# Ten value products of the second wide attention, moved into the rounds of the token attention

## The reference

```
# layer 1, ffn: token attention (16 heads of 8, keys are the 256 tokens), then 8 experts
x = x + layernorm(attention(x, Wq, bq, Wk, bk, Wv, bv, Wo, bo), ln1_g, ln1_b)
x = x + layernorm(moe(x, gate_w, gate_b, W1, b1, W2, b2), ln2_g, ln2_b)
# layer 2, attention: 16 heads of 64, keys and values from the context
xn = layernorm(x, ln_gamma, ln_beta)
q = xn @ w_q
k, v = split(context @ w_kv)
attn = softmax(q * SCALE @ k.T)
out = (attn @ v) @ w_out + b_out
```

## Time and profile before

| | us |
|---|---|
| median of three runs | 602.95 |
| profiled execution | 600.79 |
| its span | 598.7 |
| TensorE busy | 527.3 |
| VectorE busy | 449.2 |
| ScalarE busy | 344.9 |
| POOL busy | 217.3 |

### The profile page before, as it was taken

One profiled execution on the slowest core, in us unless ns is written; L12 is line 12 of the kernel. 1 busy time (PEld: TensorE's weight loads), 2 busy tenths in 40 slices (PEclk: granted clock), 3 DMA queues, 4 the chain that ended last, 5 costly groups with the idle time before them and its releaser, 6 DMA issues.

```text
span 598.7 us, 13027 instructions
## 1 busy us (share of the span) xinstructions
PE 527.3 (88%) x4784; PEld 304.3 (51%) x4792; DVE 449.2 (75%) x1251; ACT 344.9 (58%) x672; POOL 217.3 (36%) x214
## 2 busy tenths in 40 slices
PE   8889999997878799988996789688999999898896
PEld 3345555555843123333333467435666566754584
DVE  5989999998368679927876799867777776496653
ACT  3578888887144156644751768448888878222112
POOL 2047777778120000000002547206777778200100
PEclk9989999999999779999998999989999999999969
DMA  8770000004010000000000211000000000000000
GB/s 220 144 210 2 3 1 2 2 2 142 2 36 0 2 1 2 1 2 2 1 1 18 88 54 54 2 1 1 1 2 2 2 2 2 2 1 1 1 0 19
DMA packets 24082, 15.40 MB, mean 26 GB/s; under 512 B 8083, under 2 KB 22230, under 8 KB 23894
## 3 DMA queue, kind: packets, MB, share of 16 engines
q1 hardware_dynamic: 24022, 14.60, 9.2%
HBM read 14.33 MB, written 0.26 MB: 24 GB/s over the span
## 4 chain that ended last, share of the span: by engine, by line
PE 40%; issue 29%; DVE 18%; ACT 9%; POOL 3%; DMA 0%; DVEq 0%; POOLq 0%; ACTq 0%
PE psM L433 4%; PE pspair L483 3%; DVE Zt L1524 3%; ACT PP L1181 3%; PE pspair L632 3%; PE pspair L885 2%; PE psS L457 2%; PE psO L657 2%; PE psO L501 2%; DVE Oall L1782 2%; PE psS L405 2%; PE pspair L373 2%; DVE Oall L1572 1%; ACT PP L1165 1%; PE pspair L405 1%
## 5 line engine op out<-in xcount | busy, mean ns | idle before, releaser
L2193 POOL TENSOR_TENSOR ln_rs<-ln_ve,minus_half 128x4 f32<-128x4 f32 x10 | 10.2, 1023 | 225.0 <-DVE ln_ve L1411 221.8
L483 PE MATMUL pspair<-ident,PP 128*128 128x128 f32 x528 | 84.0, 282 | 7.8 <-ACT PP L1181 4.3
L483 PEld LDWEIGHTS pspair<-ident,PP 128*128 128x128 f32 x528 | 57.4, 140 | 50.5 <-issue 41.9
L501 PE MATMUL psO<-V,PP 128*128 128x64 f16 x1536 | 65.0, 193 | 11.7 <-DVE Oall L1572 9.8
L501 PEld LDWEIGHTS psO<-V,PP 128*128 128x128 f16 x1536 | 60.3, 98 | 17.1 <-DVE PP L1537 13.4
L1537 DVE TENSOR_TENSOR PP<-pspair,PP 128x512 f16<-128x512 f32 x68 | 46.8, 688 | 27.5 <-ACT PP L1165 27.4
L1239 ACT ACTIVATE PP<-pspair 128x1024 f32<-128x1024 f32 x48 | 46.6, 1023 | 30.3 <-PE pspair L643 30.2
L1181 ACT ACTIVATE PP<-scores_m,nm 128x512 f32<-128x512 f32 x68 | 49.5, 728 | 17.5 <-DVE nm L1511 13.9
L2202 POOL TENSOR_TENSOR PP<-acc,one 128x512 f16<-128x512 f32 x32 | 33.3, 1039 | 72.0 <-ACT acc L1163 71.8
L1165 ACT CAST PP<-pspair 128x512 f16<-128x512 f32 x68 | 39.6, 583 | 4.5 <-PE pspair L483 4.5
L2202 POOL TENSOR_TENSOR PP<-y_sb,one 128x512 f16<-128x512 f32 x32 | 33.3, 1039 | 19.5 <-ACT y_sb L1163 19.4
(11 more groups left out here) (497 smaller groups left out, 1224.8 us busy)
## 6 DMA issues: line engine op xcount, KB each, us to landing
W<-in_L_ffn_W SPq DMA_DIRECT2D x16, 256.0 KB, 2.9
bigw<-in_L_xattn_w_q SPq DMA_DIRECT2D x2, 512.0 KB, 5.7
bigw<-in_L_xattn_w_kv SPq DMA_DIRECT2D x1, 1024.0 KB, 5.6
V<-in_ctx SPq DMA_DIRECT2D x1, 512.0 KB, 3.9
bigw<-in_L_xattn_w_v SPq DMA_DIRECT2D x1, 512.0 KB, 5.9
mask_b<-in_mask_BxS_ff SPq DMA_DIRECT2D x1, 512.0 KB, 8.1
bigw<-in_L_xattn_w_k SPq DMA_DIRECT2D x1, 512.0 KB, 6.4
bigw<-in_L_xattn_w_o SPq DMA_DIRECT2D x1, 512.0 KB, 4.0
```

The source lines that it names most:

```text
L483: mm = pe.transpose(bank[f"T{j % 2}"][:, k * P:(k + 1) * P], Pb[j % 4][:, k * P:(k + 1) * P], ident[:])
L501: mm = pe.matmul(bank["O"][:, (j % UPH) * a.dv:(j % UPH + 1) * a.dv], (PTH, PTL)[ppart][j % 4][:, k * P:(k + 1) * P], values_of(a)[vpart][ ...
```

## The change

Products 6 to 15 are no longer made in `pe_l2x`. They are made in the rounds of the token attention, at the end of TensorE's order in the round, through the ring: one in each of rounds 0 to 5 and two in rounds 6 and 7 (`LATE_VALUES`). ScalarE, at the end of its order in the round, copies the product whole, in fp32, to one of two tiles of `scores_m` (`V32`), and that frees the bank. From the third of these copies on it first waits until POOL has split the product two before. POOL forms both halves from the fp32 copy, with two operations like those that it has for probabilities: a multiplication by one that rounds to fp16, and a subtraction. All ten splits stand in POOL's order ahead of the reciprocal root of the norm that follows the token attention. VectorE's ten subtractions are gone, and so are ScalarE's ten roundings. Ahead of the wide attention's rounds TensorE waits for all ten splits.

```diff
--- before.py
+++ after.py
@@ -93,6 +93,7 @@
 HR = P // HG
 VR = DN + 1
 MSCALE = 64.0
+LATE_VALUES = {0: (6,), 1: (7,), 2: (8,), 3: (9,), 4: (10,), 5: (11,), 6: (12, 13), 7: (14, 15)}
 L1X = Packed("L1x", SK, mask=True)
 L1F = Packed("L1f", S, scale=float(DN) ** -0.5)
 
@@ -308,6 +309,7 @@
         KW = maskf.bitcast(F16)
         zero_m = [Zt[:].bitcast(BF16)[:, k * SK:(k + 1) * SK] for k in range(2)]
         P32 = [t[:].rearrange("p t d -> p (t d)") for t in (acc, y_sb)]
+        V32 = [Sm[2], Sm[3]]
         Kst = [KW, Amat[:, 0:8, :].rearrange("p a c -> p (a c)").bitcast(F16)]
         K32 = tmp[:].rearrange("p t d -> p (t d)")
         minus16 = G[:, 0, 0, :].bitcast(F16)
@@ -538,6 +540,8 @@
                     scores(0, j)
             for v in last_v:
                 emptied(pe, v)
+            if a is L2X:
+                pe.wait_ge(sem("L2.vsplit"), 2 * NC - 6)
             run(pe, a, rounds)
             nr = a.units // UPI
             for j in range(a.lag, 0, -1):
@@ -704,6 +708,10 @@
                     turn_out(g - 1)
                 if r + a.lead < a.rounds:
                     natural(r + a.lead, 1)
+                for v in LATE_VALUES.get(r, ()) if not a.mask else ():
+                    ps, done = ring(pe, a, f"L2.V{v}")
+                    pe.matmul(ps[:], ctxT[:, v // 2 * P:(v // 2 + 1) * P], bigw[:, 2, v % 2 * 512:(v % 2 + 1) * 512],
+                              start=True, stop=True).then_inc(done, 1)
 
         def pe_out(pe, a, W, chunks):
 
@@ -906,11 +914,10 @@
             rounds(E // 2 - 1, True)
 
         def pe_l2x(pe):
-            pe_wide_values(pe, "L2", range(6, 2 * NC))
             pe_first_keys(pe, L2X, ctxT, "ld.L2")
             pe_ln(pe, "L2x", XN[1])
             pe_first_query(pe, L2X, XT[1])
-            pe_attention(pe, L2X, ctxT, XT[1], [f"L2.V{v}" for v in range(2 * NC)])
+            pe_attention(pe, L2X, ctxT, XT[1], [f"L2.V{v}" for v in range(6)])
             pe.wait_ge(sem("ld.L2wo"), 16)
             pe_out(pe, L2X, lambda c: bigw[:, 3, c * P:(c + 1) * P], NPAIR)
 
@@ -1258,6 +1265,11 @@
                     if g > 1:
                         filled(act, f"{n}.ot{g - 2}")
                     nc.scalar.copy(Osb, bank["O"][:]).then_inc(sem(f"{n}.out"), 1)
+                for v in LATE_VALUES.get(r, ()) if not a.mask else ():
+                    ps = filled(act, f"L2.V{v}")
+                    if v >= 8:
+                        act.wait_ge(sem("L2.vsplit"), v - 7)
+                    nc.scalar.copy(V32[v % 2], ps[:]).then_inc(free_of(f"L2.V{v}"), 1)
 
         def act_out(act, a, chunks):
             for c in range(0, chunks, 2):
@@ -1343,7 +1355,6 @@
             act_out(act, L1F, 1)
             act_copy(act, "L1g.xt", XT[0][:])
             act_moe(act)
-            act_wide_values(act, "L2", range(6, 2 * NC))
             act_first_keys(act, L2X)
             act_copy(act, "L2x.xt", XT[1][:])
             act_first_query(act, L2X)
@@ -1870,14 +1881,12 @@
                 add_up(E // 2 - 1, 1)
                 emptied(dve, "moe.y1", E // 2 - 1)
                 dve.wait_ge(sem("L1g.added"), 2)
-                ln_gain("L1gn", acc, "L1_ffn_ln2_g", lambda t: X[:, t, :], X, "L1gn.xn", lows("L2", range(6, 7)))
+                ln_gain("L1gn", acc, "L1_ffn_ln2_g", lambda t: X[:, t, :], X, "L1gn.xn")
                 dve.wait_ge(sem("L1gn.xn"), NT)
 
             def l2x():
                 ln_gain("L2b", X, "L2_xattn_ln_gamma", lambda t: rowp["L2_xattn_ln_beta"], XN[1], "L2x.xn",
-                        lows("L2", range(7, 8)), twice_normed=True)
-                for step in lows("L2", range(8, 16)):
-                    step()
+                        twice_normed=True)
                 first_keys(L2X)
                 first_query(L2X)
                 attention(L2X)
@@ -2272,6 +2281,18 @@
             selectors()
             rstd("L1x")
             rstd("L1f")
+
+            def split_values(v):
+                emptied(pool, f"L2.V{v}")
+                cols_ = slice(v % 2 * 512, (v % 2 + 1) * 512)
+                pool.tensor_tensor(VH[:, v // 2, cols_], V32[v % 2], one[:].broadcast_to([P, 512]), ALU.mult)\
+                    .then_inc(sem("L2.vhigh"), 1)
+                pool.wait_ge(sem("L2.vhigh"), v - 5)
+                pool.tensor_tensor(VL[:, v // 2, cols_], V32[v % 2], VH[:, v // 2, cols_], ALU.subtract)\
+                    .then_inc(sem("L2.vsplit"), 1)
+
+            for v in range(6, 2 * NC):
+                split_values(v)
             rstd("L1fn")
 
             def split_W2(i, k2, first):
```

## The result

The changed kernel took 614.02 us (median of four runs, 612.31 to 618.75), the kernel before 603.43 us (four runs, 601.65 to 603.97). The ratio is 1.0198, 95% interval 1.0155 to 1.024: slower, by an amount of which it is not clear whether it is above 2%. Ratios and their intervals leave out runs that took over 1.5% longer than the fastest of their kernel; medians leave out none. The forecast was 606.0 us, range 601.4 to 610.0: the sign was right, the size was not.

What follows compares the result with a forecast made beforehand. TensorE, busy 88% of the span, was taken as the bound: +8.2 us in the rounds, -8.2 behind the experts, +3.0 for the clock, so +3.0 on the 602.95 us median gives 606.0 us; own range 604 to 608, wider 601.4 to 610.0.

Steps and rivals of the forecast that it cites:

- the tail of the sum: Behind the rounds, TensorE's 0.99 us wait for VectorE's last normalization absorbs some 0.5 us of the delay.
- rival 4: POOL holds ScalarE at product 14 or 15, the output copy queued behind: 608 us, chance 0.07.
- The rounds: Token attention: ten products add 4.4 us in rounds 0 to 3, 1.7 in 4 and 5, 2.6 in 6 and 7.
- The bound of 10: Upper bound, in us, on the lengthening by products put into the eight rounds, forecast at 8.2.
- the wait named in the step: Rounds 0 to 3: TensorE's product waits for ScalarE's copy of the repeated query or key, making rounds 4.8 us.
- The removal with the clock: Behind the experts, taking products out saves 8.2 us; low clock at the wide attention's start costs 3.0 us.
- One reading in it: Each TensorE hole like the 3.09 us one is followed by 1.2 GHz, the packed attention at 202 to 216 included.
- The signs of being wrong: Rounds growing under 6 us, clock 1.00 at the wide attention's start, or experts' end to query's low half shrinking under 6.
- 1: Rival: products hide partly in the rounds, 6.6 us longer, and the clock returns early: 602.9 us, chance 0.20.
- 3: Rival: VectorE sets the rounds, TensorE's stalls take up products, growth 3.8 us: 599.5 us, chance 0.08.
- 2: Rival: the clock stays low for 12 us at the wide attention's start, costing 6 us: 609 us, chance 0.15.

Runs made afterwards that it cites:

- e0: The changed kernel run again without any edit, in a second job: 612.83 us, ratio 1.0169 to the kernel before.
- e2b: Changed kernel, POOL's splits on 4 columns in place of 512, zeros set during layer 1's packed attention: 606.08 us, ratio 1.0055 to the kernel before.
- e5: Changed kernel with VectorE's two expert weight splits moved from behind the rounds into round 6: 606.53 us, ratio 1.0069 to the kernel before.
- e9: Changed kernel with the product and its copy ahead of the repeated query or key in rounds 0 to 3: 617.46 us, ratio 1.0191.
- e1b: Changed kernel with products 6 to 15 and their splits left out, zeros set during layer 1's packed attention: 598.83 us, ratio 0.9922 to the kernel before.
- e4: Changed kernel with 26 filler matmuls ahead of the wide attention's transposes: 613.66 us, ratio 1.0205 to the kernel before.
- e6: Changed kernel without fillers in rounds 1 to 7, expert weight splits in round 6, 26 fillers before the wide attention's transposes: 604.38 us, ratio 0.9997.
- e10: Changed kernel with only products 12 to 15 moved, expert weight splits in round 6, key products ahead of value products 6 to 11: 600.99 us, ratio 0.9959.
- e8: Changed kernel with expert weight splits in round 6 and 26 fillers before the wide attention's transposes, rounds' fillers kept: 606.42 us, ratio 1.0017.

## Why the prediction was wrong

- **The step that failed** is the tail of the sum: "VectorE starts that work as early as before, so some 0.5 of the delay is absorbed; not all, because POOL now works beside it." I had the neighbours right and the price wrong. The weight splits took two to over three times as long, the hole went from 0.99 to 4.08 us (+3.1 in place of -0.5), and behind the hole the output product, the gate and the first expert ran at the low clock (0.50 from 329.54 to 345.5 in e0; before the change it is low from about 325 to 332), +1.4 and +2.4. The sum had no term for that clock. Hole and clock together are 6.9 us against -0.5, shown by e2b (POOL's work taken away) and by e5 (VectorE's moved): they bring 3.5 and 3.7, 6.4 and 6.4, 57.9 and 57.3 back. The clock's part scatters, +0.9 and +1.7 in the first execution for the +1.4 and +2.4 of e0, while the hole is 4.08 us in both. In the spans the miss is 9.2 us (12.2 against 3.0): 7.4 from the tail and what follows it, 0.9 from the rounds ahead of the tail, -0.3 from the removal, 1.2 from the rest. In the medians it is 7.6 (10.6 against 3.0).
- The rule on shared interfaces (the Trainium skill, "GPSIMD Engine Reference", Specifications: contention with VectorE's instructions that have two SBUF inputs or run in a two-port mode) stood beside rival 4, ScalarE held by POOL. The traces agree with it: two SBUF operands (0.69 to 1.41 and 1.64 us) were hit, reductions from PSUM in the rounds (0.68) were not. The cast (0.41 to 1.34) was hit too; whether it runs in a two-port mode no run here shows. I asked what it does to POOL, and not what it does to VectorE's instruction on the path.
- **The rounds**: forecast +8.7 ahead of the tail, measured +9.6. 4.8 us a round was 4.82 to 4.95 in rounds 0 to 2, and 5.48 in round 3, which was longer before too (4.32). Rounds 0 to 3 grew by 5.0 us together (forecast 4.4; four times 1.14 is 4.6, not 4.4), rounds 4 and 5 by 2.2 (1.7), rounds 6 and 7 by 2.4 (2.6). The bound of 10 stood for the sum with the tail, and that is 12.7: it does not hold. Whether the wait named in the step makes its length is open, since e9 removed it and brought others.
- **The removal with the clock**: forecast -8.2 + 3.0 = -5.2, measured -5.5 in the trace, and e1b shows it by itself (-5.4). The clock's part is 2.6 us by e4, against 3.0, and without it e4 has 8.0 saved, against 8.2. This step was right in its parts. One reading in it was not: no hole of 3 us stands ahead of the low clock at 202, where TensorE was idle for 0.2 to 0.6 us at a time, so a low clock does not always follow a long hole.
- **The signs of being wrong** that the prediction named did not appear: the rounds grew by more than 6 us, the clock was low at the start of the wide attention, and the experts' end to the query's low half shrank by 6.9 us, from 20.8 to 13.9. None of them looked at the tail.
- **Rivals.** 1 and 3 (products hidden in the rounds) are out: +9.6. 2 (12 us of low clock at the attention's start) is not what happened: in e0 the clock is back at full by 414, ahead of the attention's first transposes at 415.97, and costs 2.6 us. 4 does not act in the changed kernel, whose ScalarE waits 0.41 us there, and does in e6.
- **What stays open.** The last 1.6 us, from the first transposed probabilities to the end, differ from execution to execution (the same stretch takes 192.1 us in e4 and 195.0 in the first execution), and I have no experiment on them. Nor is it shown why the experts in e6 had low clock that e5 did not. So of the +2.4 in the experts, that the hole brought all of it is argued from e2b and e5, and e6 speaks against it.

## What to carry to other kernels

Ask of work that is to move whether it cost anything where it stood: six of these ten products filled a hole. With only the other four moved, the weight splits earlier and the key products ahead, the kernel took 0.3% less than before, where moving all ten had lost 2%. A helper engine's load is not free because nobody waits for it: look up what VectorE does beside POOL at that time, and whether its instruction is on the path. And a new hole of 4 us on TensorE was paid twice here, the second time in the clock of what follows.

## What was not expected of the hardware

- VectorE and POOL slow each other: VectorE's fp32 to fp16 cast of 512 columns from 0.41 to 1.34 us, its subtraction from 0.69 to 1.41, four normalizations of 128 columns from 1.11 to 4.96 us beside a memset of POOL. POOL's splits went from 1.04 to 1.22 and from 1.16 to 1.49 us. VectorE's reductions from PSUM kept their 0.68 us.
- Executions of one kernel differ by up to 2.3%, and the longer ones have the lower mean clock (e10 594.3 us at 0.974 to 608.0 at 0.939, e1b 594.6 to 603.2, e8 599.6 to 609.6). The kernel before is mostly within 601.5 to 606 us, and from 600.3 to 609.3 in the job of e6. Stage lengths told these kernels apart where medians of four runs did not: the rounds took 37.14 or 37.15 us in e0, e2b, e4 and e5. They too need a look at the clock: the same rounds took 38.79 us at 0.96 and 40.19 at 0.89.
